# Squares and normalisation of queries and keys moved from GpSimd to VectorE in a one-core layer of attention and experts

## The chip, the cores and the metric

The kernel runs on one core of one Trainium2 chip. The metric is the device time of the kernel in microseconds, from one launch to its end; lower is better. A core has TensorE (PE, and PEld for its weight loads), VectorE (DVE), ScalarE (ACT), GpSimd (POOL) and SyncE (SP), which work side by side, each through its own list of instructions in program order. They wait for one another only on semaphores.

## What is computed

One layer over 16 sequences of 256 tokens with 128 features. The input is layer-normalised; two branches, a linear attention with random features and a mixture of soft-routed experts, are added to it.

```python
xn = _layernorm(x)                                   # 16 x 256 x 128
qkv = xn @ Wqkv + bqkv;  q, k, v = split(qkv, 3)     # 16 heads of 8
# features of q and of k:
u    = t / max(norm(t, axis=-1), 1e-12)              # per head of 8 numbers
proj = einsum('bhtd,rhdm->rbhtm', u, omega)          # 2 x 32 features
feat = exp(clip(proj * sqrt_2s - s, -20, 20)) / sqrt(32) * sqrt(weights)
# causal linear attention:
ctx = sum over earlier tokens of (q_f . k_f) v ;  den = max(sum (q_f . k_f), 1e-6)
attn = (ctx / den) @ Wout + bout
# soft mixture: logits of tokens and 512 slots, softmax over experts and over slots
slots = dispatch^T xn;  h = gelu(slots @ w1);  processed = h @ w2
ffn = combine @ processed
out = x + attn + ffn
```

The change touches `u`: the division of every head of 8 numbers of `q` and `k` by its norm.

## The kernel before

One pass of the loop (`row`, numbered 0 to 15 here) handles one sequence. Its 256 tokens lie as two tiles of 128. Every engine has its own `row` function, in which the steps stand in the order written by hand; nothing else sets the order. Passes 0 and 1 and the last two are written out, the twelve between run in a hardware loop of two passes (`run_rows`). In each function `b` is the pass, `b1` the next, `b2` the one after, `bp` the one before. Work is staggered: while pass `b` runs through the experts, its engines prepare queries, keys and values of `b1` and finish the attention of `bp`.

Queries and keys of `b1` go this way in pass `b`:

- TensorE makes `x23` = qkv (`qkv_product`), VectorE adds the bias and scales into `qkv` (`qkv_bias`, L758).
- `squares` (L322) writes `qk_sq` = qkv times qkv, 128x512. In the loop GpSimd does it. For pass 0, ahead of the loop, VectorE does.
- VectorE sums eights (`qk_norms`, L764) and applies a floor (L767).
- ScalarE takes the inverse root as Exp(-0.5 Ln) (`qk_root`, L525 and L527), and VectorE sharpens it with a Newton step of three instructions (`qk_newton`, L709, L711, L713, on 64 columns).
- `qk_apply` (L327) writes `qk_n` = qkv times the inverse norm, 128x512. In the loop on GpSimd, ahead of it on VectorE.
- ScalarE copies `qk_n` into `stack` in 16 bits (`stack_high`, L546), GpSimd writes the remainder (`stack_low`, L335), ScalarE copies once more (L677), SyncE turns the stack by a transposing DMA (`turn_stack`), and TensorE projects it in pass `b1` (`project`, L1014).

Around it: VectorE and ScalarE take score blocks out of PSUM (`evac_a`, L787, and `evac_b`, L559), GpSimd then multiplies half of them by a causal mask (`mask_b`, L476). VectorE's `slots_low` is L837, `clip` L781, `ctx_norm` starts with L795; `ln_newton` uses L709, L711 and L713 on four columns. ScalarE's functions Exp and Ln are in one table and Gelu is in another, so that a table load (L671) stands ahead of `gelu`. Its order in that part is

```python
evac_b(b, 2)
qk_root(b1)
evac_b(b, 3)
nc.scalar.preload_act_table_set(GELU)
gelu(b, 0)
stack_high(b1)
gelu(b, 1)
```

TensorE's `processed_low` (L1176) waits for `gelu(b, 0)`. In front of it stand `hidden` and `project(b, 2)`, `project(b, 3)`, and these two wait for `evac_a` and `evac_b` of blocks 2 and 3.

Of the kernel before, what the change touches and what calls it, by code (L numbers as in the profile page):

```python
# [34 lines left out]
def count(b, per, extra):  # L35

    i, u = b
    if isinstance(i, int):
        return (2 * i + u) * per + extra
    return i * (2 * per) + (u * per + extra)  # L40
# [8 lines left out]
def after(eng, sem, value):  # L49

    if isinstance(value, int) and value <= 0:
        return
    eng.wait_ge(sem, value)


def hold(eng, sem, value):

    if isinstance(value, int) and value <= 0:
        return
    eng.wait_ge(sem, value)  # L60
    eng.nop(nofuse=True)
# [7 lines left out]
def step(b, k):  # L69

    i, u = b
    u += k
    return (i + u // 2, u % 2)
# [19 lines left out]
def build(nc, x, Wqkv, bqkv, Wout, bout, omega, nodes, weights, gamma_x, gamma_slot, slot_embeds,  # L93
          w1, w2, out):
    with ExitStack() as ctx:
# [224 lines left out]
        def squares(eng, b):  # L320
            hold(eng, qkvs_ok, count(b, 1, 1))
            eng.tensor_tensor(qk_sq[:, :, :], qkv[:, :, 0:256], qkv[:, :, 0:256], ALU.mult).then_inc(sq_ok, 1)  # L322

        def qk_apply(eng, b):
            hold(eng, qk_nw, count(b, 3, 3))
            rn = small[:, NT, :].rearrange("p (j h a) -> p j h a", j=2, a=1).broadcast_to([128, 2, 32, HD])
            eng.tensor_tensor(qk_n[:, :, :].rearrange("p j (h d) -> p j h d", d=HD),  # L327
                              qkv[:, :, 0:256].rearrange("p j (h d) -> p j h d", d=HD), rn,
                              ALU.mult).then_inc(qkn_ok, 1)

        def stack_low(eng, b):
            hold(eng, sthi_ok, count(b, 1, 1))
            hold(eng, d_st, count(b, 16, 0))
            hold(eng, qkn_ok, count(b, 1, 1))
            eng.tensor_tensor(stacked(1), parted(), stacked(0), ALU.subtract).then_inc(stlo_ok, 1)  # L335
# [80 lines left out]
        def _(pool):  # L416
# [30 lines left out]
            def residual(b):  # L447

                hold(pool, d_x[b[1]], landed(b, 1))
                hold(pool, o1_ok, count(b, 1, -1))  # L450
                pool.tensor_tensor(xres[:, b[1], :, :], xin[:, b[1], :, :],
                                   bout_bc[:, :].rearrange("p (a c) -> p a c", a=1).broadcast_to([128, TILES, C]),
                                   ALU.add).then_inc(xr_ok, 1)

            def place_v(b):
                hold(pool, qkvs_ok, count(b, 1, 1))
                hold(pool, cx_ok, count(b, 4, -4))
                for a in range(4):
                    heads = slice(QUADS * a, QUADS * a + QUADS)
                    c = 256 + 32 * a  # L460
                    last = pool.tensor_copy(vw[:, b[1], :, heads, v_col(a):v_col(a) + HD],
                                            qkv[:, :, c:c + 32].rearrange("p j (h d) -> p j h d", d=HD))
                last.then_inc(v_ok, 1)

            def mask_pair(b, p):
                hold(pool, ev_ok, count(b, 2, p - 5))
                v = s_sb[:, p, :, :].rearrange("p k (a t) -> p k a t", t=128)[:, :, 0:3:2, :]
                m = causal[:, :].rearrange("p (k a t) -> p k a t", k=1, t=128)[:, :, 0:3:2, :].broadcast_to(
                    [128, 2, 2, 128])
                pool.tensor_tensor(v, v, m, ALU.mult).then_inc(mb_ok, 1)  # L470

            def mask_b(b, p):
                hold(pool, eb_ok, count(b, 6, p + 1))
                v = s_sb[:, p, 1, :].rearrange("p (a t) -> p a t", t=128)[:, 0:3:2, :]
                m = causal[:, :].rearrange("p (a t) -> p a t", t=128)[:, 0:3:2, :]
                pool.tensor_tensor(v, v, m, ALU.mult).then_inc(mb_ok, 1)  # L476
# [17 lines left out]
            def row(b, first, nxt, nxt2):  # L494
                b1, bp = step(b, 1), step(b, -1)
                if not first:
                    mask_pair(bp, 6)
                    mask_pair(bp, 7)
                if nxt:
                    residual(b1)  # L500
                    squares(pool, b1)
                mask_b(b, 0)
                mask_b(b, 1)
                if nxt:
                    qk_apply(pool, b1)
                    stack_low(pool, b1)
                mask_b(b, 2)
                mask_b(b, 3)
                if nxt:
                    place_v(b1)  # L510
                mask_b(b, 4)
                mask_b(b, 5)
# [192 lines left out]
        def _(dve):  # L705
            def newton(src, y, t, w, done, base, extra):

                ys, ts = small[:, y, 0:w], small[:, t, 0:w]
                nc.vector.scalar_tensor_tensor(ts, ys, -0.5, ys, ALU.mult, ALU.mult).then_inc(done, 1)  # L709
                after(dve, done, count(base, 3, extra - 2))  # L710
                nc.vector.tensor_tensor(ts, ts, small[:, src, 0:w], ALU.mult).then_inc(done, 1)  # L711
                after(dve, done, count(base, 3, extra - 1))
                nc.vector.scalar_tensor_tensor(ts, ts, 1.5, ys, ALU.add, ALU.mult).then_inc(done, 1)  # L713
                after(dve, done, count(base, 3, extra))
# [47 lines left out]
            def qk_norms(b):  # L762
                after(dve, sq_ok, count(b, 1, 1))
                nc.vector.tensor_reduce(small[:, NQ, :], qk_sq[:, :, :].rearrange("p j (h d) -> p (j h) d", d=HD),  # L764
                                        AX_X, ALU.add).then_inc(red_ok, 1)
                after(dve, red_ok, count(b, 2, 1))
                nc.vector.tensor_scalar(small[:, NM, :], small[:, NQ, :], NORM_FLOOR, None,  # L767
                                        ALU.max).then_inc(red_ok, 1)

            def qk_newton(b):  # L770
                after(dve, qk_a, count(b, 2, 2))
                after(dve, red_ok, count(b, 2, 2))
                newton(NM, NY, NT, 64, qk_nw, b, 3)
# [45 lines left out]
            def slot_maxima(b):  # L819

                for h in range(2):
                    after(dve, lt_ok, count(b, 2, h + 1))
                    nc.vector.tensor_reduce(maxima[:, 2 * h:2 * h + 2], x23[:, h, :].rearrange("p (c t) -> p c t", t=T),  # L823
                                            AX_X, ALU.max).then_inc(mx_ok, 1)
# [34 lines left out]
            b0, b1 = (0, 0), (0, 1)  # L859
# [47 lines left out]
            def row(b, first, nxt, nxt2):  # L907

                b1, b2, bp = step(b, 1), step(b, 2), step(b, -1)
                token_maxima(b)  # L910
                if first:
                    ln_stats(b1)
                slot_maxima(b)
                if first:
                    dve.wait_ge(f_ln, 1)
                    nc.vector.tensor_tensor(f_bias[:, :], coef_ln[:, :], node_c[:, :], ALU.subtract).then_inc(f_ok, 1)
                    ln_newton(b1)
                    ln_scale(b1)
                elif nxt2:
                    ln_stats(b2)  # L920
                clip(b, 0)
                slots_norm(b, 0)
                slots_norm(b, 1)
                if first:
                    xt_low(b1)
                clip(b, 1)
                if first:
                    ln_stats(b2)
                if first:
                    slots_low(b)  # L930
                if nxt:
                    qkv_bias(b1)
                evac_a(b, 0)
                evac_a(b, 1)
                if not first:
                    slots_low(b)
                if nxt:
                    qk_norms(b1)
                evac_a(b, 2)
                evac_a(b, 3)  # L940
                if nxt:
                    qk_newton(b1)
                if nxt2:
                    ln_newton(b2)
                if nxt2:
                    ln_scale(b2)
                clip(b, 2)
                if not first and nxt:
                    ctx_norm(bp)
                clip(b, 3)  # L950
                if nxt:
                    add_experts(b)
                else:
                    ctx_norm(bp)
                if nxt2:
                    xt_low(b2)
                if not first and nxt:
                    add_attention(bp)
                evac_a(b, 4)
                evac_a(b, 5)  # L960
# [366 lines left out]
```

## Time and profile before

| | before |
|---|---|
| median of 3 runs | 450.51 us (449.58 to 450.86) |
| the profiled execution | 450.92 us |
| its span, first to last instruction | 449.2 us |
| mean granted TensorE clock | 0.995 |
| TensorE (matmul) busy | 431.4 us, 96% |
| VectorE busy | 348.2 us, 78% |
| ScalarE busy | 319.3 us, 71% |
| GpSimd busy | 188.8 us, 42% |

The span is what the instructions cover in the profiled execution; the 1.7 us beside it lie around them. Busy time is a share of the whole span and doesn't say who waits for whom: for that the timelines below are read. In a line of a timeline stand the start and the length in us, the engine, the line of the kernel, the operation, what it writes and reads, the shapes, and how many instructions were merged into it. In brackets, if anything, the idle time of the engine ahead of it and who ended it. A start can lie a little ahead of the end of the instruction before on the same engine, since they overlap in the pipeline.

### The profile page before, as it was taken

The page shows a single profiled execution, that of the slowest core. Times are in us where ns is not written, and L with a number is a line of the kernel's source. Part 1 is how long each engine was busy: PE and PEld are TensorE (multiplying, and loading weights), DVE is VectorE, ACT ScalarE, POOL GpSimd, SP SyncE. Part 2 cuts the span into 40 slices and gives each one's busy share as a digit, 9 for nine tenths or more (in the row PEclk, how much of TensorE's full clock was granted, in tenths as well). Part 3 has the DMA queues.
Part 4 walks back from the last instruction along what each step waited for, and adds up shares of the span by engine and source line. Part 5 has one row for each costly group of instructions (what it writes and reads, how often), then busy time and mean ns, then how long its engine had stood idle before and what let it go on. Part 6 is the DMA issues. An engine that isn't in the chain of part 4 may idle for free.

```text
span 449.2 us, 15766 instructions
## 1 busy us (share of the span) xinstructions
PE 431.4 (96%) x5724; PEld 361.5 (80%) x5724; DVE 348.2 (78%) x872; ACT 319.3 (71%) x530; POOL 188.8 (42%) x280
## 2 busy tenths in 40 slices
PE   6688999999999999999999999999999999999986
PEld 3467888898888889888888988888898888889775
DVE  7797797978778697877969787796978779576643
ACT  4458686877958687685868768586876858676671
POOL 5605454344445434434643443464344346434310
PEclk9899999999999999999999999999999999999999
DMA  4302003030200203020020302002030201103001
GB/s 108 88 25 49 14 4 60 14 60 16 47 26 8 51 12 58 12 47 23 13 46 12 58 12 47 23 17 41 12 58 12 47 12 24 36 1 61 2 1 25
DMA packets 45307, 14.37 MB, mean 32 GB/s; under 512 B 35360, under 2 KB 45152, under 8 KB 45280
## 3 DMA queue, kind: packets, MB, share of 16 engines
q1 hardware_dynamic: 44432, 13.48, 14.6%
q10 hardware_dynamic: 720, 0.53, 0.4%
q8 instruction: 17, 0.28, 0.2%
q0 software_dynamic: 128, 0.01, 0.1%
q14 instruction: 10, 0.08, 0.1%
HBM read 3.44 MB, written 2.10 MB: 12 GB/s over the span
## 4 chain that ended last, share of the span: by engine, by line
PE 90%; DVE 6%; ACT 2%; issue 1%; POOL 0%; DVEq 0%; ACTq 0%; POOLq 0%
PE x L979 19%; PE p_s L1029 10%; PE p_t L1029 8%; PE x L1176 7%; PE x L1144 7%; PE x L1185 6%; PE x L1197 6%; PE x L1042 5%; PE p_s L1042 5%; PE x L1117 3%; PE p_s L1014 2%; PE x L1128 2%; PE x L1093 2%; PE x L1152 2%; PE x L1136 1%; PE x L1081 1%
## 5 line engine op out<-in xcount | busy, mean ns | idle before, releaser
L476 POOL TENSOR_TENSOR s_sb<-s_sb,causal 128x256 f32<-128x256 f32 x96 | 68.5, 734 | 82.5 <-ACT s_sb L559 82.4
L553 ACT ACTIVATE feat<-arg,f_bias 128x1024 f32<-128x1024 f32 x64 | 71.7, 1147 | 8.0 <-DVE arg L781 8.0
L781 DVE TENSOR_SCALAR arg<-p_s,f_low,f_high 128x1024 f32<-128x1024 f32 x32 | 42.9, 1340 | 18.6 <-PE p_s L1014 12.1
L1029 PEld LDWEIGHTS p_s<-feat 64*64 64x64 f32 x1024 | 38.8, 132 | 17.4 <-issue 15.8
L322 POOL TENSOR_TENSOR qk_sq<-qkv 128x512 f32<-128x512 f32 x15 | 15.6, 1042 | 86.8 <-DVE qkv L758 86.8
L1029 PE MATMUL p_s<-feat 64*64 64x256 f32 (+3 forms) x1024 | 49.5, 309 | 1.6 <-ACT feat L553 1.6
L470 POOL TENSOR_TENSOR s_sb<-s_sb,causal 128x512 f32<-128x512 f32 x30 | 37.6, 1276 | 26.5 <-ACT s_sb L565 26.5
L1029 PE MATMUL p_t<-feat 64*64 64x256 f32 (+3 forms) x1024 | 47.1, 299 | 0.0
L781 DVE TENSOR_SCALAR arg<-p_t,f_low,f_high 128x1024 f32<-128x1024 f32 x32 | 42.7, 1335 | 0.0
L1029 PEld LDWEIGHTS p_t<-feat 64*64 64x64 f32 x1024 | 41.3, 133 | 1.5
L1176 PEld LDWEIGHTS x<-w_sb,hid_t 128*128 128x128 f32 x256 | 29.8, 191 | 8.5 <-ACT hid_t L593 8.0
L1144 PEld LDWEIGHTS x<-xg,disp 128*128 128x128 f32 x256 | 29.8, 191 | 7.9 <-ACT disp L581 7.9
L559 ACT ACTIVATE s_sb<-p_s 128x384 f32<-128x384 f32 x48 | 23.6, 491 | 15.8 <-PE p_s L1029 15.8
L1176 PE MATMUL x<-w_sb,hid_t 128*128 128x128 f32 x256 | 32.8, 281 | 1.7 <-ACT hid_t L593 1.7
L823 DVE TENSOR_REDUCE maxima<-x 128x2 bf16<-128x512 f32 x32 | 20.6, 686 | 17.0 <-PE x L1117 16.9
L1144 PE MATMUL x<-xg,disp 128*128 128x129 f32 x256 | 32.8, 281 | 0.2
L593 ACT ACTIVATE hid_t<-x 128x1024 f32<-128x1024 f32 x32 | 32.7, 1021 | 0.3
L565 ACT ACTIVATE s_sb<-p_s 128x768 f32<-128x768 f32 x15 | 12.2, 813 | 28.2 <-PE p_s L1029 28.2
L1197 PE MATMUL x<-proc,comb_t 128*128 128x129 f32 x256 | 31.6, 275 | 0.0
L1185 PE MATMUL x<-w_sb,hid_t 128*128 128x128 f32 x256 | 31.2, 275 | 0.0
L1197 PEld LDWEIGHTS x<-proc,comb_t 128*128 128x128 f32 x256 | 29.9, 191 | 0.3 <-issue 0.2
L1185 PEld LDWEIGHTS x<-w_sb,hid_t 128*128 128x128 f32 x256 | 29.8, 192 | 0.0
(162 smaller groups left out, 1038.9 us busy)
## 6 DMA issues: line engine op xcount, KB each, us to landing
xin<-in_L_attn_x_dram SPq DMA_DIRECT2D x31, 64.0 KB, 2.3
out_dram<-out_sb SPq DMA_DIRECT2D x31, 64.0 KB, 2.1
se_rows<-n_L_ffn_slot_embeds_dram SPq DMA_DIRECT2D x1, 256.0 KB, 4.1
w_f<-in_L_ffn_w_dram SPq DMA_DIRECT2D x1, 256.0 KB, 4.0
w_sb<-in_L_ffn_w_dram SPq DMA_DIRECT2D x1, 256.0 KB, 3.9
stack_t<-stack SPq DMA_TRANSPOSE x16, 4.3
wqkv_f<-in_L_attn_Wqkv_dram ACTq DMA_DIRECT2D x1, 192.0 KB, 2.9
bqkv_bc<-in_L_attn_bqkv_dram ACTq DMA_DIRECT2D x1, 192.0 KB, 4.9
```

The lines of the kernel that those rows point to most:

```text
L470: pool.tensor_tensor(v, v, m, ALU.mult).then_inc(mb_ok, 1)
L476: pool.tensor_tensor(v, v, m, ALU.mult).then_inc(mb_ok, 1)
L553: nc.scalar.activation(feat[:, k:k + 2, :], arg[:, k:k + 2, :], ACT.Exp, bias=f_bias[:, 0:1]).then_inc(fe_ok, 1)
L593: nc.scalar.activation(hid_t[:, 2 * half:2 * half + 2, :], (x01, x23)[half][:, :, :], ACT.Gelu).then_inc(ge_ok, 1)
L781: nc.vector.tensor_scalar(arg[:, k:k + 2, :], (p_s, p_t)[g % 2][:, :, :], f_low[:, 0:1], f_high[:, 0:1], ALU.max, ALU.min).then_inc(cl_ok, 1)
L979: mm = nc.tensor.matmul(dst, a, w, start=start and i == 0, stop=stop and i == 2, skip_group_check=True)
L1029: mm = nc.tensor.matmul(dst[rows:rows + 64, u, o:o + hi - lo], f[:, T + keys:T + keys + 64], f[:, lo:hi], start=True, stop=True, skip_grou ...
L1042: mm = nc.tensor.matmul(dst[32 * q:32 * q + 32, j, :], vw[:, b[1], kt, QUADS * a + q, :], s_sb[:, p, q % 2, o:o + 128], start=(kt == 0 and ...
L1144: mm = nc.tensor.matmul(x01[:, half, 129 * (c % 2):129 * (c % 2) + 129], disp[:, j, 128 * c:128 * c + 128], xg[:, b[1], j, :], start=(j == ...
L1176: nc.tensor.matmul(x01[:, c // 2, o:o + 128], hid_t[:, m, 128 * c:128 * c + 128], w2_sb[:, m, :], start=(m == 0 and c % 2 == 0), stop=Fals ...
L1185: mm = nc.tensor.matmul(x01[:, c // 2, o:o + 128], hid_t[:, m, 128 * c:128 * c + 128], w2_sb[:, m, :], start=False, stop=(m == 3), skip_gr ...
L1197: mm = nc.tensor.matmul(x23[:, 0, 129 * j:129 * j + 129], comb_t[:, c, 128 * j:128 * j + 128], proc[:, c, :], start=(c == 0 and j == 0), s ...
```

## The change

On VectorE, `squares` now stands behind `evac_a(b, 1)` and, in all passes but 0, `slots_low`, directly in front of `qk_norms`. `qk_apply` stands directly behind `qk_newton`, in front of `ln_newton` of the pass after next. Both are gone from GpSimd's list. The instructions are the same, in operands and shape; only the engine and the place differ. Both helpers begin with an explicit wait and an empty instruction (`hold`).

```diff
@@ GpSimd, row
                 if nxt:
                     residual(b1)
-                    squares(pool, b1)
                 mask_b(b, 0)
                 mask_b(b, 1)
                 if nxt:
-                    qk_apply(pool, b1)
                     stack_low(pool, b1)
                 mask_b(b, 2)
                 mask_b(b, 3)
@@ VectorE, row
                 if not first:
                     slots_low(b)
                 if nxt:
+                    squares(dve, b1)
                     qk_norms(b1)
                 evac_a(b, 2)
                 evac_a(b, 3)
                 if nxt:
                     qk_newton(b1)
+                    qk_apply(dve, b1)
                 if nxt2:
                     ln_newton(b2)
```

VectorE's list in a pass before, from the second evacuation to the four-column Newton (`small` holds the norms and roots, `s_sb` the evacuated scores):

```order
L787 TENSOR_TENSOR s_sb<-p_t,causal 128x384
L837 TENSOR_TENSOR slot_lo<-x,slot_hi 128x512
L764 TENSOR_REDUCE small<-qk_sq 128x64
L767 TENSOR_SCALAR small<-small 128x64
L787 TENSOR_TENSOR s_sb<-p_s,causal 128x384
L787 TENSOR_TENSOR s_sb<-p_t,causal 128x384
L709 SCALAR_TENSOR_TENSOR small<-small 128x64
L711 TENSOR_TENSOR small<-small 128x64
L713 SCALAR_TENSOR_TENSOR small<-small 128x64
L709 SCALAR_TENSOR_TENSOR small<-small 128x4
```

Here the sums (L764) follow `slots_low` (L837) directly, and one Newton step the other. The same piece after the change, whose line numbers are two lower from the edit on:

```order
L785 TENSOR_TENSOR s_sb<-p_t,causal 128x384
L835 TENSOR_TENSOR slot_lo<-x,slot_hi 128x512
L322 TENSOR_TENSOR qk_sq<-qkv 128x512
L762 TENSOR_REDUCE small<-qk_sq 128x64
L765 TENSOR_SCALAR small<-small 128x64
L785 TENSOR_TENSOR s_sb<-p_s,causal 128x384
L785 TENSOR_TENSOR s_sb<-p_t,causal 128x384
L707 SCALAR_TENSOR_TENSOR small<-small 128x64
L709 TENSOR_TENSOR small<-small 128x64
L711 SCALAR_TENSOR_TENSOR small<-small 128x64
L327 TENSOR_TENSOR qk_n<-qkv,small 128x512
L707 SCALAR_TENSOR_TENSOR small<-small 128x4
```

The squares have come between `slots_low` and the sums, ahead of the floor; the multiply has come between the two Newton steps.

GpSimd's list at the same place of a pass, as a difference from before:

```order
 L470 TENSOR_TENSOR s_sb<-s_sb,causal 128x2x2x128 x2
 L451 TENSOR_TENSOR xres<-xin,bout_bc 128x256
-L322 TENSOR_TENSOR qk_sq<-qkv 128x512
 L476 TENSOR_TENSOR s_sb<-s_sb,causal 128x2x128 x2
-L327 TENSOR_TENSOR qk_n<-qkv,small 128x512
 L335 TENSOR_TENSOR stack<-qk_n,stack 128x32x16
 L476 TENSOR_TENSOR s_sb<-s_sb,causal 128x2x128 x2
```

The masks 0 and 1 (L476) no longer stand behind the squares, and `stack_low` (L335) follows them directly. The lists of TensorE, ScalarE and SyncE are unchanged.

## Rows read from the trace of the kernel before

**Rows 1.** The page's busy time; busy time by stretch (columns: PE, PEld, DVE, ACT, POOL, PEclk).

```profile
PE 431.4 (96%) x5724; PEld 361.5 (80%) x5724; DVE 348.2 (78%) x872; ACT 319.3 (71%) x530; POOL 188.8 (42%) x280
...
30.00:40.00 10.00, 7.76 (x92) 5.79 (x91) 9.33 (x27) 7.16 (x13) 3.98 (x5) 1.00 0.00 0
```

**Rows 2.** Timeline of pass 7, TensorE's weight loads for `processed_low`.

```profile
220.53 1.64 PEld L1176 LDWEIGHTS x<-w_sb,hid_t 128*128 128x128 f32 x14 [0.42 <-ACT hid_t L593]
```

**Rows 3.** Timeline of pass 7, VectorE: `slots_low`, sums, floor, four-column Newton, `ctx_norm`.

```profile
215.34 0.68 DVE L837 TENSOR_TENSOR slot_lo<-x,slot_hi 128x512 fp32r<-128x512 f32 x1
215.94 0.68 DVE L764 TENSOR_REDUCE small<-qk_sq 128x64 f32<-128x512 f32 x1
216.65 0.46 DVE L767 TENSOR_SCALAR small<-small 128x64 f32<-128x64 f32 x1
...
218.90 1.03 DVE L709 SCALAR_TENSOR_TENSOR small<-small 128x4 f32<-128x4 f32 x1 [0.21 <-DVE small L713]
...
223.05 0.27 DVE L795 TENSOR_SCALAR den<-x 128x16 f32<-128x16 f32 x2 [0.47 <-PE x L1081]
```

**Rows 4.** Timeline of pass 7, ScalarE: second evacuation, logarithm, first Gelu.

```profile
215.23 0.48 ACT L559 ACTIVATE s_sb<-p_t 128x384 f32<-128x384 f32 x1
...
217.14 0.26 ACT L525 ACTIVATE small<-small 128x64 f32<-128x64 f32 x1
...
219.38 1.02 ACT L593 ACTIVATE hid_t<-x 128x1024 f32<-128x1024 f32 x1
```

**Rows 5.** Timeline of pass 7, GpSimd: squares, masks 0 and 1, multiply.

```profile
214.64 1.04 POOL L322 TENSOR_TENSOR qk_sq<-qkv 128x512 f32<-128x512 f32 x1 [5.40 <-DVE qkv L758]
215.63 1.42 POOL L476 TENSOR_TENSOR s_sb<-s_sb,causal 128x256 f32<-128x256 f32 x2
218.83 1.08 POOL L327 TENSOR_TENSOR qk_n<-qkv,small 128x512 f32<-128x512 f32 x1 [1.78 <-DVE small L713]
```

**Rows 6.** Timeline of pass 0: ScalarE, VectorE and TensorE's loads, engine by engine.

```profile
32.98 0.48 ACT L559 ACTIVATE s_sb<-p_t 128x384 f32<-128x384 f32 x1
...
37.72 1.02 ACT L593 ACTIVATE hid_t<-x 128x1024 f32<-128x1024 f32 x1
...
34.77 0.68 DVE L767 TENSOR_SCALAR small<-small 128x64 f32<-128x64 f32 x1
...
37.07 0.16 DVE L709 SCALAR_TENSOR_TENSOR small<-small 128x4 f32<-128x4 f32 x1
...
38.79 1.30 PEld L1176 LDWEIGHTS x<-w_sb,hid_t 128*128 128x128 f32 x11 [2.11 <-ACT hid_t L593]
```

**Rows 7.** Timeline of pass 8: ScalarE, VectorE and TensorE's loads, engine by engine.

```profile
241.45 0.48 ACT L559 ACTIVATE s_sb<-p_t 128x384 f32<-128x384 f32 x1
...
245.51 1.03 ACT L593 ACTIVATE hid_t<-x 128x1024 f32<-128x1024 f32 x1
...
241.47 0.68 DVE L837 TENSOR_TENSOR slot_lo<-x,slot_hi 128x512 fp32r<-128x512 f32 x1
...
242.78 0.46 DVE L767 TENSOR_SCALAR small<-small 128x64 f32<-128x64 f32 x1
...
246.70 0.41 PEld L1176 LDWEIGHTS x<-w_sb,hid_t 128*128 128x128 f32 x3 [0.42 <-ACT hid_t L593]
```

**Rows 8.** Timeline of the prologue: VectorE's squares, floor, multiply; GpSimd's addition.

```profile
10.84 0.69 DVE L322 TENSOR_TENSOR qk_sq<-qkv 128x512 f32<-128x512 f32 x1
...
12.29 0.20 DVE L767 TENSOR_SCALAR small<-small 128x64 f32<-128x64 f32 x1
...
15.62 0.72 POOL L451 TENSOR_TENSOR xres<-xin,bout_bc 128x256 f32<-128x256 f32 x1
...
15.88 1.02 DVE L327 TENSOR_TENSOR qk_n<-qkv,small 128x512 f32<-128x512 f32 x1
```

**Rows 9.** Timeline ahead of pass 7: ScalarE's evacuation and GpSimd's pair of masks.

```profile
202.29 0.49 ACT L559 ACTIVATE s_sb<-p_s 128x384 f32<-128x384 f32 x1 [0.46 <-PE p_s L1029]
...
202.93 1.44 POOL L476 TENSOR_TENSOR s_sb<-s_sb,causal 128x256 f32<-128x256 f32 x2 [4.51 <-ACT s_sb L559]
```

## The prediction

> **What bounds the kernel now.** I read the page first, then the granted clock by stretches, then the timelines of single passes of the loop. TensorE is busy 96% of the span [rows 1], and most of the chain that ended last is its own. So an edit on VectorE and GpSimd costs or gives only where TensorE waits for something behind it, and the question is which wait that is. The edited work is squares of queries and keys, their sums, a floor, a root on ScalarE, Newton steps, and the multiply. In the timelines of pass 7 the reader can follow who hangs on the floor (L767). It ends at 217.11 [rows 3] and ScalarE's logarithm (L525) starts at 217.14 [rows 4]: no slack. ScalarE works in program order: behind the root stand one evacuation, a table load and the Gelu of the first half, 219.38 to 220.40. TensorE's weight loads for `processed_low` (L1176) start at 220.53, released by that Gelu [rows 2]. How much room is in those 0.13 us? In pass 0, where TensorE truly waited (2.11 us), the load came 0.05 us after the Gelu's end (37.72 + 1.02 = 38.74, load 38.79) [rows 6]. So pass 7 has 0.08 us of room. Pass 8 ends its Gelu at 246.54 and loads at 246.70: room 0.11 us [rows 7]. **A later floor is a later TensorE, in every pass with a next row, less about 0.1 us.**
>
> **Squares, removed from GpSimd.** L322 on GpSimd takes 1.04 us, 214.64 to 215.68 [rows 5]. It ran beside two evacuations and `slots_low` on VectorE, which end only at 215.34 + 0.68 = 216.02 [rows 3]. The sums started at 215.94, straight behind them, and waited for no square. So the removed 1.04 us lay wholly beside other work and gives VectorE nothing back at this place.
>
> **Squares, added to VectorE.** The same instruction ran once on VectorE in the prologue, with GpSimd idle: 0.69 us [rows 8]. In the loop it stands between `slots_low` and the sums, on the chain above. It meets company, because GpSimd's masks come earlier once the squares are gone from its queue. When GpSimd is idle, a mask starts about 0.14 us after its evacuation by ScalarE ends: 202.29 + 0.49 = 202.78, and the mask at 202.93 [rows 9]. In pass 7 the second evacuation ends at 215.71 [rows 4], so the second mask runs from 215.85 for 0.73 us (a pair takes 1.42, slightly overlapped [rows 5]) to 216.58. VectorE reaches the squares at about 216.05. What does a VectorE instruction with two operands in SBUF do while GpSimd multiplies SBUF by SBUF? Two rows answer. L709 on four columns takes 0.16 us alone [rows 6] and 1.03 us when it starts 0.07 us behind GpSimd's `qk_n`, ending 0.02 us after it (219.93 against 218.83 + 1.08 = 219.91) [rows 3, 5]. The prologue's L327, a multiply of the very size of the squares, started at 15.88 under GpSimd's addition (15.62 to 16.34) and ended at 16.90, 0.56 us after it [rows 8]. So I let the squares end 0.56 us after the mask.
>
> The new chain from the end of ScalarE's second evacuation is then 0.14 (to the mask) + 0.73 (mask) + 0.56 (squares) + 0.04 (to the sums) + 0.68 (sums [rows 3]) + 0.04 + 0.20 (floor) = 2.39 us. The 0.04 is the gap that sums and floor leave now (215.94 + 0.68 to 216.65 [rows 3]), and 0.20 is the floor's free length in the prologue [rows 8]; in the loop it takes 0.46, as the mask holds it, and that is gone too. **Pass 7**: 215.71 + 2.39 = 218.10 against 217.11, 0.99 late, 0.91 after the room. **Pass 8**: the evacuation ends at 241.93, so 244.32 against 242.78 + 0.46 = 243.24, 1.08 late, 0.97 after the room [rows 7]. The odd passes look like pass 7, the even ones like pass 8. **Pass 0**: the evacuation ends at 33.46, so 35.85 against 34.77 + 0.68 = 35.45: 0.40 late with no room, since TensorE waits there anyway [rows 6]. Pass 15 has no next row and nothing changes. The sum is 7 x 0.91 + 7 x 0.97 + 0.40 = 13.6 us.
>
> Bounds of the added squares: from below 0.69 us without any block; from above the whole 0.69 behind the mask instead of 0.56, which adds 0.13 x 15 = 2 us.
>
> The Trainium skill has the rule: in "SBUF — State Buffer", section "Who interferes with whom", a VectorE instruction with two SBUF inputs contends with a GpSimd instruction that reads SBUF, and whichever issues first holds the shared pair for its whole length. By it the squares would start only at the mask's end and take their full length, 13.6 + 2 = 15.6 us. The row of L327 ended sooner, so the measurement decides for 0.56.
>
> **Multiply, removed from GpSimd and added to VectorE.** On GpSimd `qk_n` ran 218.83 to 219.91 [rows 5]. On VectorE it stands behind the Newton steps. GpSimd is idle by then, its next step waits for ScalarE's `stack_high`, so no block: between the 0.69 us of the squares' size and the 1.02 us that L327 took under a block [rows 8]; I take 0.7, since nothing contends. Measured from the same late floor, `qk_n` is ready no later than before (218.9 + 0.7 = 219.6 against 219.91). Its reader, ScalarE's copy, stands behind the Gelu that ends at 220.40 [rows 4], so even 1.02 us is covered; without that cover each 0.1 us would be another 0.1 us on ScalarE. On VectorE it pushes the four-column Newton by 0.7 us and takes away the 0.87 us for which GpSimd's `qk_n` held it (1.03 against 0.16). Net -0.1 to +0.2 us ahead of `clip(b, 2)`. Behind it VectorE waits 0.47 us for TensorE's transposes (L795 [rows 3]), which covers that. **Cost nothing.**
>
> **What else waits.** The evacuations `evac_a` 2 and 3 come about 1 us later. Today they and the 64-column Newton are over by 218.9, where the four-column one starts [rows 3]; `project(b, 2)` and `(b, 3)` want them just ahead of L1176, at about 220, so they still come in time. `stack_low` on GpSimd waits for the same ScalarE copy as before. Masks 0 and 1 come earlier, for nobody. No DMA is moved; the stack's transpose on SP shifts with ScalarE as TensorE does, and its reader stands in the next pass.
>
> Nothing gives the lateness back: ScalarE's whole queue behind the root moves with it, and TensorE's later waits in the pass are for that queue or for its own results. Does TensorE's clock hold? Between 30 and 40 us it was busy only 7.76 of 10 us and was granted 1.00 [rows 1], so another 0.9 us of idling should not change it.
>
> The profiled execution took 450.92 us (span 449.2 and 1.7 us around it), 0.4 above the median 450.51. 450.92 + 13.6 - 0.4 = 464.1; I say **464.0 us**.
>
> **Rivals.** (1) *VectorE reaches the squares before the mask.* Then the mask waits and the squares take 0.69. How near is it? If the squares need no time beyond the queue, they start where the sums do now: 215.94 against the mask's 215.85 in pass 7, and 242.07 against 242.07 in pass 8. The explicit wait ahead of the squares should add some 0.1 us: the sums, which have no such step, start 0.08 us before `slots_low` ends, and an engine that runs an extra empty instruction first (my estimate) loses that overlap. That speaks for the mask, and 0.07 us behind was enough for L709 to be held. Price: 216.05 + 0.69 + 0.04 + 0.68 + 0.04 + 0.20 = 217.70, 0.59 late, 0.5 after the room; 14 x 0.5 + 0.4 = 7.4, so 457.9 us if in all passes, 461 if only in the even ones.
>
> (2) *Lateness absorbed* (not slower). If `processed_low` were really held by the projections in front of it and the root's chain had a microsecond of slack, or if TensorE's stall shortened its later waits, the added 0.69 us would vanish: 450.5 us. For it: TensorE's matmuls fill 96% of the span, so little of this wait shows as idle. Against: the loads follow the Gelu by only 0.13 and 0.16 us [rows 2, 7].
>
> (3) *Faster.* If what TensorE waits for is not the Gelu but VectorE's second half (`xg`, `clip(b, 2)`, `ctx_norm`), then ending the block of 0.87 us for a multiply of 0.7 gives 0.15 us in each of 14 passes: 450.5 - 2.1 = 448.4 us. It decides only where VectorE arrives last; the wait of 0.47 us at L795 says it does not. The Trainium skill leans this way: "GPSIMD Engine Reference", section "Engine selection", sends elementwise work on two inputs to VectorE since GpSimd is about twice as slow. The rows agree on the ratio (1.04 against 0.69), but it prices the instruction, not its place.
>
> (4) *Worse than forecast*: the clock falls, or a second stall opens, for instance at `attn_back`: 467 us and more.
>
> **How the numbers follow.** Forecast (mask first in nearly all passes, 462 to 466) 0.62; rival 1, in part or whole, 457 to 462, 0.20; absorbed 0.08; faster 0.04; worse 0.06. The range reaches from rival 1 in all passes, with 1 us for its terms, to the full block: 457 to 467, leaving out under 0.2. A measurement of this kernel tells 0.3% (1.4 us) from no change. Faster 0.04, same 0.07, slower 0.89.
>
> **What would show it.** In the changed profile: VectorE's L322 near 1.1 us (0.53 waiting for the mask and 0.56) and not 0.69; the floor near 0.2; ScalarE's L525 waiting some 1 us for it; loads of L1176 with idle of 1.3 us in place of 0.42, released by the Gelu; a pass of 27.1 us in place of 26.17 (220.53 to 246.70); the four-column Newton at 0.16. Wrong if L1176 waits as before, if L322 takes 0.69, or if the pass stays at 26.2.

## The result and the profile after

The changed kernel took 462.12 us (median of 4 runs, 461.98 to 462.27) against 450.69 us for the kernel before, run beside it: a ratio of 1.0253, 95% interval 1.0224 to 1.0281. It is 11.4 us slower; 13.5 us were forecast, with a range of 457 to 467. The profiled execution took 461.99 us with a span of 460.3 us.

The page of the changed kernel, its busy times and three of its groups (columns: instructions, busy us, mean ns of one, idle us ahead and who ended it):

```profile
PE 434.2 (94%) x5724; PEld 363.2 (79%) x5724; DVE 357.1 (78%) x902; ACT 319.6 (69%) x530; POOL 162.2 (35%) x250
...
L476 POOL TENSOR_TENSOR s_sb<-s_sb,causal 128x256 f32<-128x256 f32 x96 | 72.4, 769 | 175.3 <-ACT s_sb L557 175.3
...
L1176 PEld LDWEIGHTS x<-w_sb,hid_t 128*128 128x128 f32 x256 | 31.4, 200 | 17.9 <-ACT hid_t L591 17.5
...
L1176 PE MATMUL x<-w_sb,hid_t 128*128 128x128 f32 x256 | 34.4, 290 | 10.3 <-ACT hid_t L591 10.3
```

TensorE's share fell from 96% [rows 1] to 94%, GpSimd's from 42% to 35%, and VectorE stays at 78% of a longer span. GpSimd gave away 27 us of work for which another engine had waited only once, VectorE for 0.29 us in pass 0. TensorE's idle time ahead of L1176 is where the loss is: the matmuls there waited 1.7 us for the Gelu in the whole kernel before, all of it in pass 0, and 10.3 us now.

Pass 7 of the changed kernel, VectorE first, then ScalarE, GpSimd and TensorE's loads (timeline; it answers to rows 2 to 5; line numbers from the edit on are two lower):

```profile
220.84 0.68 DVE L835 TENSOR_TENSOR slot_lo<-x,slot_hi 128x512 fp32r<-128x512 f32 x1
221.44 1.20 DVE L322 TENSOR_TENSOR qk_sq<-qkv 128x512 f32<-128x512 f32 x1
222.67 0.69 DVE L762 TENSOR_REDUCE small<-qk_sq 128x64 f32<-128x512 f32 x1
223.39 0.19 DVE L765 TENSOR_SCALAR small<-small 128x64 f32<-128x64 f32 x1
...
225.36 0.69 DVE L327 TENSOR_TENSOR qk_n<-qkv,small 128x512 f32<-128x512 f32 x1
225.97 0.15 DVE L707 SCALAR_TENSOR_TENSOR small<-small 128x4 f32<-128x4 f32 x1
...
229.46 0.27 DVE L793 TENSOR_SCALAR den<-x 128x16 f32<-128x16 f32 x2 [0.69 <-PE x L1081]
...
223.62 0.26 ACT L523 ACTIVATE small<-small 128x64 f32<-128x64 f32 x1 [1.01 <-DVE small L765]
...
225.86 1.02 ACT L591 ACTIVATE hid_t<-x 128x1024 f32<-128x1024 f32 x1
...
221.36 0.73 POOL L476 TENSOR_TENSOR s_sb<-s_sb,causal 128x256 f32<-128x256 f32 x1 [0.68 <-ACT s_sb L557]
...
226.93 1.86 PEld L1176 LDWEIGHTS x<-w_sb,hid_t 128*128 128x128 f32 x16 [1.33 <-ACT hid_t L591]
```

The mask starts at 221.36, the squares 0.08 us behind it. The mask ends at 222.09 and the squares at 222.64, 0.55 us later: they were held. ScalarE then waits 1.01 us for the floor, and TensorE's loads 1.33 us for the Gelu. They had idled 0.42 us before [rows 2], under matmuls that were still running; the matmuls of L1176 themselves idled 0.00 us before and 0.84 us now. The multiply takes 0.69 us and the four-column Newton behind it 0.15 us, where it had been held for 1.03 [rows 3].

Pass 8 of the same profile, VectorE, GpSimd and TensorE's loads:

```profile
248.48 0.68 DVE L322 TENSOR_TENSOR qk_sq<-qkv 128x512 f32<-128x512 f32 x1
...
249.91 0.20 DVE L765 TENSOR_SCALAR small<-small 128x64 f32<-128x64 f32 x1
...
248.48 1.27 POOL L476 TENSOR_TENSOR s_sb<-s_sb,causal 128x256 f32<-128x256 f32 x1 [0.68 <-ACT s_sb L557]
...
253.45 1.86 PEld L1176 LDWEIGHTS x<-w_sb,hid_t 128*128 128x128 f32 x16 [0.77 <-ACT hid_t L591]
```

Here both start at 248.48 and VectorE wins. The squares take their free 0.68 us, and the mask, 0.73 alone, takes 1.27. TensorE's loads wait only 0.77 us. Six of the 14 later passes with a next row (2, 4, 6, 8, 10, 12) went this way, eight (the odd ones and pass 14) the other. The mean of the mask group shows it too: 769 ns against 734 before, and 6 x 0.54 us over 96 masks is 34 ns.

Distance between the first loads of L1176 in neighbouring passes, from the timelines:

| kernel | into pass 7 | into pass 8 |
|---|---|---|
| before | 26.06 | 26.17 |
| the whole change | 26.97 | 26.52 |
| squares only | 26.98 | 26.51 |
| multiply only | 26.06 | 26.16 |
| change, mask 1 behind the squares | 26.55 | 26.62 |
| change, block 3 evacuated first | 26.60 | 26.17 |
| change, mask 1 behind the floor, block 3 first | 26.06 | 26.16 |
| before, block 3 first | 26.07 | 26.15 |
| change, multiply twice | 26.95 | 26.52 |
| squares twice | 26.67 | 26.74 |

### The profile page after: what moved, and what is told of

Same layout as the page of the kernel before. It is cut to its first block, busy times and chain, and to the rows that moved or that the text cites. A ratio compares the mean times of both kernels' runs of the same rounds, so it can differ in the third digit from the quotient of the medians.

```text
span 460.3 us, 15753 instructions
## 1 busy us (share of the span) xinstructions
PE 434.2 (94%) x5724; PEld 363.2 (79%) x5724; DVE 357.1 (78%) x902; ACT 319.6 (69%) x530; POOL 162.2 (35%) x250
## 4 chain that ended last, share of the span: by engine, by line
PE 61%; DVE 19%; ACT 9%; issue 8%; DMA 1%; DVEq 1%; ACTq 0%
PE x L1176 7%; PE x L979 7%; PE x L1144 7%; PE x L1185 6%; PE x L1197 6%; PE p_s L1029 5%; PE p_s L1042 5%; PE p_t L1029 4%; ACT hid_t L591 3%; PE x L1117 3%; DVE qk_sq L322 3%; DVE qkv L756 3%; ACT L669 3%; DVE small L762 2%; DVE s_sb L785 2%
## 5 line engine op out<-in xcount | busy, mean ns | idle before, releaser
L476 POOL TENSOR_TENSOR s_sb<-s_sb,causal 128x256 f32<-128x256 f32 x96 | 72.4, 769 | 175.3 <-ACT s_sb L557 175.3
L1029 PEld LDWEIGHTS p_s<-feat 64*64 64x64 f32 x1024 | 38.8, 132 | 17.4 <-issue 15.9
L470 POOL TENSOR_TENSOR s_sb<-s_sb,causal 128x512 f32<-128x512 f32 x30 | 37.6, 1276 | 26.8 <-ACT s_sb L563 26.8
L1176 PEld LDWEIGHTS x<-w_sb,hid_t 128*128 128x128 f32 x256 | 31.4, 200 | 17.9 <-ACT hid_t L591 17.5
L335 POOL TENSOR_TENSOR stack<-qk_n,stack 128x512 f16<-128x512 f32 x15 | 17.5, 1165 | 77.2 <-ACT stack L544 77.2
L1176 PE MATMUL x<-w_sb,hid_t 128*128 128x128 f32 x256 | 34.4, 290 | 10.3 <-ACT hid_t L591 10.3
L1144 PE MATMUL x<-xg,disp 128*128 128x129 f32 x256 | 32.8, 281 | 0.2
L1185 PE MATMUL x<-w_sb,hid_t 128*128 128x128 f32 x256 | 31.2, 275 | 0.0
L1185 PEld LDWEIGHTS x<-w_sb,hid_t 128*128 128x128 f32 x256 | 29.9, 192 | 0.0
```

Source lines behind the costliest of these rows:

```text
L1029: mm = nc.tensor.matmul(dst[rows:rows + 64, u, o:o + hi - lo], f[:, T + keys:T + keys + 64], f[:, lo:hi], start=True, stop=True, skip_grou ...
L1144: mm = nc.tensor.matmul(x01[:, half, 129 * (c % 2):129 * (c % 2) + 129], disp[:, j, 128 * c:128 * c + 128], xg[:, b[1], j, :], start=(j == ...
L1176: nc.tensor.matmul(x01[:, c // 2, o:o + 128], hid_t[:, m, 128 * c:128 * c + 128], w2_sb[:, m, :], start=(m == 0 and c % 2 == 0), stop=Fals ...
L1185: mm = nc.tensor.matmul(x01[:, c // 2, o:o + 128], hid_t[:, m, 128 * c:128 * c + 128], w2_sb[:, m, :], start=False, stop=(m == 3), skip_gr ...
```

## Where the 11.1 us of span went

By the first loads of L1176 in both profiles, the loss adds up to the difference of the spans. Passes into which the mask came first: 0.91 us each for 3, 5, 7, 9, 11 and 13, 0.93 for 14 and 0.95 for 1 (by the profile of the squares alone, whose clock was full there), together 7.3. Passes where VectorE came first: 0.32 to 0.35 each, together 2.0. Pass 0: 0.14 as the profiles stand; it holds 0.25 us by which this execution came earlier to the loop (see **Pass 0** below). That is 9.5 us. The remaining 1.6 us is TensorE's clock, once. This is TensorE of the changed kernel by stretches around its wait in pass 0 (columns: us, PE busy, granted clock, DMA share, GB/s):

```profile
36.00:38.00 2.00, 1.04 (x6) 1.00 0.00 0
38.00:39.00 1.00, 0.07 (x1) 0.95 0.00 0
39.00:42.00 3.00, 3.00 (x14) 0.50 0.00 0
42.00:43.00 1.00, 1.00 (x10) 0.85 0.92 171
```

From 39 to 42 us it was granted half of the full clock (1.2 GHz in place of 2.4), just behind the wait for the first Gelu. Of the 16 matmuls of L1176 in pass 0, thirteen took 0.42 us each by their own length in place of 0.28, which is why the group L1176 is busy 34.4 us in place of 32.8. The profile of the kernel before had the same wait (2.11 us [rows 6]) and kept its full clock there.

## The experiments

Each kernel was profiled and then timed beside the kernel before on the same chip. In the first set of four the kernel before had a median of 451.29 us (14 runs), in the second 451.12 us (19 runs). All single times move by 1 to 3 us with the mean granted clock of the run: the kernel before took 449.5 to 449.9 us at 0.998 to 0.999 and 452.6 to 453.1 at 0.986 to 0.987. Part of this lies ahead of the loop. The profile of the kernel before was below the full clock there (columns as above):

```profile
15.00:20.00 5.00, 2.72 (x8) 0.80 0.08 18
20.00:25.00 5.00, 4.39 (x27) 0.85 0.65 128
```

It reached the first load of L1176 at 38.79 us. The profiles with the full clock up to there reached it at 37.1 to 37.8, the ones without at 38.8 to 39.9, whatever the kernel. So the distances between loads above, which leave all this out, carry the arguments, and the medians confirm them.

### The two halves of the change

Only the squares on VectorE, against the changed kernel:

```diff
@@ GpSimd, row
                 if nxt:
+                    qk_apply(pool, b1)
                     stack_low(pool, b1)
@@ VectorE, row
                     qk_newton(b1)
-                    qk_apply(dve, b1)
```

> Only the squares are on VectorE; the multiply stays with GpSimd, behind masks 0 and 1. My theory (all of the loss comes from the squares in front of the floor, the multiply is covered): the same as with the whole change, 462 us, within 1.5 us, with the squares again near 1.20 us in odd passes and 0.68 in even ones, and the four-column Newton again held for some 0.87 us by the multiply on GpSimd. Rival (both instructions cost VectorE their length on the path, 0.69 us each): half of the loss goes, about 456 us.

Measured: 461.57 us (ratio to before 1.0239, 1.019 to 1.0287). Pass 7, VectorE, GpSimd, loads:

```profile
220.23 1.20 DVE L322 TENSOR_TENSOR qk_sq<-qkv 128x512 f32<-128x512 f32 x1
...
224.24 1.02 DVE L708 SCALAR_TENSOR_TENSOR small<-small 128x4 f32<-128x4 f32 x1 [0.21 <-DVE small L712]
...
224.18 1.07 POOL L327 TENSOR_TENSOR qk_n<-qkv,small 128x512 f32<-128x512 f32 x1 [3.29 <-DVE small L712]
...
225.73 1.42 PEld L1176 LDWEIGHTS x<-w_sb,hid_t 128*128 128x128 f32 x12 [1.33 <-ACT hid_t L592]
```

The squares are held and TensorE's loads wait 1.33 us exactly as in the whole change, while the four-column Newton is held again by the multiply. This block of 0.87 us changes nothing for TensorE.

Only the multiply on VectorE, against the changed kernel:

```diff
@@ GpSimd, row
                     residual(b1)
+                    squares(pool, b1)
@@ VectorE, row
-                    squares(dve, b1)
                     qk_norms(b1)
```

> Only the multiply is on VectorE; the squares stay with GpSimd in front of masks 0 and 1. My theory: it costs nothing, as the Gelu that its reader stands behind ends later and the block of the four-column Newton goes: 450.7 us, within 1 us, loads of L1176 idle 0.42 us as before. Rival (both cost their length): about 456 us or, if it is all the multiply's, 462 us.

Measured: 451.66 us, ratio 1.0001 (0.9978 to 1.0023). Pass 7:

```profile
218.74 0.69 DVE L327 TENSOR_TENSOR qk_n<-qkv,small 128x512 f32<-128x512 f32 x1
219.35 0.16 DVE L708 SCALAR_TENSOR_TENSOR small<-small 128x4 f32<-128x4 f32 x1
...
220.45 1.64 PEld L1176 LDWEIGHTS x<-w_sb,hid_t 128*128 128x128 f32 x14 [0.42 <-ACT hid_t L592]
```

The multiply is free, and ending the block gains nothing either. The whole loss belongs to the squares.

### Is the 1.20 us a block?

The whole change, with mask 1 waiting for the squares:

```diff
@@ GpSimd, row
                 mask_b(b, 0)
+                if nxt:
+                    hold(pool, sq_ok, count(b1, 1, 1))
                 mask_b(b, 1)
```

> The whole change, but GpSimd waits for the squares before mask 1, so that VectorE is first in every pass. My theory (in 8 of 14 passes and in pass 0 the mask holds the squares for 0.5 us): squares 0.68 us in all passes, all passes 26.5 us, 14 x 0.35 = 5 us above before and 0.4 us back in pass 0: 455.3 us, or 457 if the clock falls in pass 0 again. Rival (the 1.20 us is VectorE's own time, not a block; only the added instruction counts): squares stay at 1.20 in odd passes and the time at 462 us.

Measured: 457.48 us (ratio 1.0144, 1.0099 to 1.0189). Pass 7, VectorE and GpSimd:

```profile
217.43 0.68 DVE L322 TENSOR_TENSOR qk_sq<-qkv 128x512 f32<-128x512 f32 x1
...
218.86 0.30 DVE L767 TENSOR_SCALAR small<-small 128x64 f32<-128x64 f32 x1
...
218.37 0.74 POOL L476 TENSOR_TENSOR s_sb<-s_sb,causal 128x256 f32<-128x256 f32 x1 [1.70 <-DVE qk_sq L322]
```

The squares take 0.68 us in every pass, so the 0.5 us was the mask's. Passes became 26.55 and 26.62 us, not the 26.5 that was expected. The rows tell why: the mask now runs from 218.37 to 219.11 over the floor, which is held until 219.16 and takes 0.30 us in place of 0.20. I had moved the collision by one instruction. In pass 14 the overlap was worse and the floor took 0.55 us. That is why 455.3 us was too low: even the profiled execution, at the full clock, took 456.42.

### Is it floor, root, table load, Gelu?

The whole change, with ScalarE's order turned, so that block 3 is evacuated in the time in which ScalarE waits for the floor:

```diff
@@ ScalarE, row
                 evac_b(b, 2)
+                evac_b(b, 3)
                 if nxt:
                     qk_root(b1)
-                evac_b(b, 3)
```

> The whole change, but ScalarE evacuates block 3 ahead of the root instead of behind it, in the time in which it waits for the floor. My theory (the path is floor, root, table load, Gelu, processed_low): the Gelu comes 0.47 us earlier against the floor, so 0.91 becomes 0.44 in the odd passes and 0.34 becomes 0 in the even ones: 8 x 0.45 and 0.3 us less in pass 0, some 454 us, 455.6 if the clock falls as with the change. Rival (VectorE as a whole is late, and the root is not what TensorE hangs on): 462 us as before.

Measured: 455.81 us (ratio 1.0102, 1.0068 to 1.0136). ScalarE in pass 7, and the loads of passes 7 and 8:

```profile
220.96 0.49 ACT L557 ACTIVATE s_sb<-p_t 128x384 f32<-128x384 f32 x1
221.91 0.26 ACT L523 ACTIVATE small<-small 128x64 f32<-128x64 f32 x1 [0.47 <-DVE small L765]
...
223.77 1.02 ACT L591 ACTIVATE hid_t<-x 128x1024 f32<-128x1024 f32 x1
...
224.85 1.30 PEld L1176 LDWEIGHTS x<-w_sb,hid_t 128*128 128x128 f32 x11 [0.94 <-ACT hid_t L591]
...
251.02 1.08 PEld L1176 LDWEIGHTS x<-w_sb,hid_t 128*128 128x128 f32 x9 [0.42 <-ACT hid_t L591]
```

From the logarithm to the Gelu it is 1.86 us in place of 2.24 (223.62 to 225.86), 0.38 earlier and not 0.47. The odd passes fell from 0.91 to 0.54 above before, the even ones to nothing. VectorE's list is unchanged, so TensorE hangs on ScalarE's queue behind the floor and not on VectorE's second half. This profile also had the clock at half behind the wait of pass 0, the one of squares only had not.

Both mends together, with the mask behind the floor (`hold(pool, red_ok, count(b1, 2, 2))` in place of the wait above) and block 3 first:

> The whole change, with GpSimd's mask 1 waiting for VectorE's floor and with ScalarE's block 3 evacuated ahead of the root. My theory (late by the added squares less the ended hold of the floor, 1.63 against 1.17 us = 0.46; 0.38 given back by ScalarE's order, 0.08 to 0.11 by the room): nothing is left, passes of 26.1 us, the time of the kernel before within 1 us, the floor at 0.20 us and loads of L1176 idle 0.42. Rival (VectorE's longer list costs by itself): at least 0.3 us a pass remains, 455 us or more.

Measured: 450.30 us, ratio 0.9982 (0.9964 to 0.9999). Pass 7, VectorE and loads:

```profile
214.29 0.69 DVE L322 TENSOR_TENSOR qk_sq<-qkv 128x512 f32<-128x512 f32 x1
...
215.73 0.20 DVE L767 TENSOR_SCALAR small<-small 128x64 f32<-128x64 f32 x1
...
218.89 1.19 PEld L1178 LDWEIGHTS x<-w_sb,hid_t 128*128 128x128 f32 x10 [0.43 <-ACT hid_t L593]
```

Nothing is left of the loss, though VectorE does all that it does in the changed kernel. The kernel before with ScalarE's order turned alone tells whether this order is a gain of its own:

> The kernel before, with only ScalarE's order turned (block 3 ahead of the root). My theory: TensorE reaches the loads of L1176 with the Gelu just done, so an earlier Gelu gives it nothing: the time of before within 1 us, so what this order gave in the changed kernel was lateness taken back. Rival (the order is a gain of its own): 5 us faster than before.

Measured: 449.85 us, ratio 0.998 (0.996 to 0.9999). Its loads in pass 7 and in pass 0:

```profile
218.88 1.30 PEld L1176 LDWEIGHTS x<-w_sb,hid_t 128*128 128x128 f32 x11 [0.42 <-ACT hid_t L593]
...
37.14 1.53 PEld L1176 LDWEIGHTS x<-w_sb,hid_t 128*128 128x128 f32 x13 [1.74 <-ACT hid_t L593]
```

The passes stay at 26.07 and 26.15 us. Only in pass 0, where TensorE truly waits, the Gelu's earlier end counts: 1.74 in place of 2.11 us. Runs at a mean clock of 0.998 and more agree: 449.1 to 449.4 us here, 449.3 with both mends, 449.5 to 449.9 for the kernel before. Both are some 0.4 us (0.1%) faster than before; the rest of the difference of medians goes with the clock of the runs. No version was found that beats the kernel before by more than that.

### Doubling one, doubling the other

The whole change, with the multiply done once more into the free `qk_sq`, ahead of the real one. In the diff `qk_again` is the multiply of `qk_apply` without wait and signal:

```diff
@@ VectorE, row
                     qk_newton(b1)
+                    qk_again(b1)
                     qk_apply(dve, b1)
```

> The whole change, with the multiply done twice on VectorE, one behind the other. My theory (qk_n ends 0.8 us ahead of the Gelu that ScalarE's copy stands behind, and VectorE waits 0.69 us for TensorE's transposes behind clip): 0.70 us more in front of both is still covered, 462 us, within 1.5 us, and the wait ahead of L793 shrinks to near 0. Rival (the multiply is on the path): 0.7 x 15 = 10 us more, 472 us.

Measured: 461.25 us (ratio 1.0216, 1.0181 to 1.0251). Pass 7, VectorE:

```profile
224.76 0.69 DVE L333 TENSOR_TENSOR qk_sq<-qkv,small 128x512 f32<-128x512 f32 x1
225.37 0.69 DVE L327 TENSOR_TENSOR qk_n<-qkv,small 128x512 f32<-128x512 f32 x1
...
228.96 0.27 DVE L798 TENSOR_SCALAR den<-x 128x16 f32<-128x16 f32 x2 [0.17 <-PE x L1087]
```

A second multiply costs nothing: the passes stay at 26.95 and 26.52 us. VectorE's wait for the transposes shrank from 0.69 to 0.17 us: that is the cover, and it is nearly used up.

The kernel with both mends, with the squares done twice (first into the spare tile `junk`, with the same wait):

```diff
@@ VectorE, row
                 if nxt:
+                    sq_again(b1)
                     squares(dve, b1)
                     qk_norms(b1)
```

> As the first kernel of this set (mask 1 behind the floor, block 3 ahead of the root), but the squares are computed twice on VectorE, the first time into a spare tile. It does work that the reference does not ask for. My theory (once the room is used up, what stands in front of the floor costs its length): 0.69 to 0.72 us a pass, 10 us above the first kernel, 461 us, passes of 26.8 us. Rival (slack elsewhere takes it): under 3 us above.

Measured: 459.81 us (ratio 1.0193, 1.0166 to 1.0221), 9.5 us above the kernel with both mends. Pass 7, VectorE and loads:

```profile
220.10 0.69 DVE L333 TENSOR_TENSOR junk<-qkv 128x512 f32<-128x512 f32 x1
220.70 0.69 DVE L322 TENSOR_TENSOR qk_sq<-qkv 128x512 f32<-128x512 f32 x1
...
225.31 1.86 PEld L1183 LDWEIGHTS x<-w_sb,hid_t 128*128 128x128 f32 x16 [1.04 <-ACT hid_t L597]
```

Two in a row overlap by 0.09 us, so the second adds 0.60 us and not the 0.69 to 0.72 of the theory, and the passes grew by 0.61 and 0.58 (26.67 and 26.74, 26.8 expected). Once the room is gone, what stands in front of the floor costs its full step, pass after pass. The profile lost another 1.6 us behind pass 0's wait, where the clock was at half.

## Why the prediction was right, and where it was off

**What bounds the kernel.** Right. Turning ScalarE's order took the even passes back to 26.17 us without an edit on VectorE, and the squares alone carried the whole loss.

**Squares: GpSimd's 1.04 us gives nothing back.** Right for the loop: with the multiply alone on VectorE and with the squares alone, TensorE's loads moved only by what came in front of the floor. In pass 0 of the kernel before, VectorE's sums did wait 0.29 us for GpSimd's squares. The forecast for pass 0 starts at the evacuation and ends at the measured floor, so it has this wait in it.

**The length of held squares.** Right to 0.01 us: 0.55 us past the mask's end, 0.56 predicted from the prologue. From the evacuation's end (221.22) to the floor's end (223.58) the chain took 2.36 us, 2.39 predicted, and the odd passes cost 0.91 us each, as predicted. The squares took 1.20 us and not 1.1, as they began to wait 0.1 us sooner. The full length behind the mask, which the Trainium skill ("SBUF — State Buffer", "Who interferes with whom") would give, was 0.14 us too long. What the Trainium skill states there besides, that the first to issue keeps the other out, agrees with the odd passes, where the mask started 0.08 us ahead. In the even passes the two starts agree to 0.01 us, and no row tells who was first.

**Who comes first in the even passes.** This is the step that failed. I took the explicit wait and its empty instruction ahead of the squares for 0.1 us, so that the mask would win everywhere. They cost nothing: the squares start 0.60 us behind the start of `slots_low` (220.84 to 221.44), just as the sums had (215.34 to 215.94 [rows 3]). Without the 0.1 us the sum in rival 1 stood at a tie in pass 8, 242.07 against 242.07, and VectorE won it, as in all six passes where the starts agree to 0.01 us. Why it wins such a tie is open. One of the prediction's own signs of being wrong, L322 at 0.69 us, came true in these six. The even passes then cost 0.34 us in place of 0.97: 6 x 0.63 = 3.8 us too much in the forecast. Rival 1 had this case, "only in the even ones", at 461 us.

**Pass 0.** The floor came 2.37 us after the evacuation's end in place of 1.99 (33.46 to 35.45 before), 0.38 later against 0.40 predicted. It cost only 0.14 us in the profile, since ScalarE reached that evacuation 0.25 us sooner, for reasons ahead of the loop. In the profile of the squares alone, where the evacuation ended at 33.46 as before, the floor and the loads of L1176 both came 0.39 us later (35.84, and 39.18 against 38.79). So the step was right.

**The multiply costs nothing.** Right, and by more than one way: alone it gives the time of before, and twice it still costs nothing.

**TensorE's clock.** Wrong. I read from one stretch with the full clock that another wait would not lower it. In the profile it fell behind pass 0's wait and cost 1.6 us. All four runs of the changed kernel had a mean clock of 0.988 to 0.991. The kernel before had 0.986 to 0.999; its profile (0.995) was below the full clock ahead of the loop and not here, and where its other runs were, no trace shows. So it isn't shown that the change makes the fall likelier: the profile of the squares alone has the same wait of pass 0 and kept the full clock. The run of the doubled multiply at 0.999 took 459.44 us, 9.5 to 9.9 more than the kernel before at 0.998 to 0.999; that is the cost of the change with the clock left out, and the 9.4 us of passes 1 to 14 with 0.4 for pass 0 give it.

**The sum.** With 3.8 us too much for the even passes, 0.3 too much for pass 0 and 1.6 too little for the clock, the sum of 13.6 us stood 2.5 above the 11.1 us of the spans. The errors leaned against each other; how near the total came is partly luck.

**Rivals.** "Absorbed" falls with the 1.33 and 0.77 us of idle ahead of L1176. "Faster" falls with the multiply alone, which ended the block of 0.87 us and gained nothing. The prediction took GpSimd's 1.04 us against 0.69 for an agreement with "about twice as slow"; it is a factor of 1.5.

## What to carry to other kernels

Before moving an instruction from an idle engine to a busy one, ask who waits for its result, not what it takes: in the loop the squares were free on GpSimd, though 1.5 times as long there, because they ended under other VectorE work, and on VectorE 0.69 us stood in front of a root, a table load and a Gelu that TensorE waits for. Taking work off GpSimd also lets its other work start sooner, here just onto the moved instruction. When a late result can't be made earlier, let its waiting engine do independent work first: one swapped line on ScalarE gave back 0.34 to 0.37 us a pass.

## What the runs showed of the hardware beyond the expected

- VectorE with two operands in SBUF and GpSimd multiplying in SBUF exclude each other both ways, though no semaphore stands between them. Started at the same time by the profile (248.48), VectorE kept 0.68 us and GpSimd's mask grew from 0.73 to 1.27, ending 0.59 us behind the squares; 0.08 us behind the mask, the squares grew to 1.20. Held work ends sooner than its full length after the release: 0.55 of 0.69 and 0.59 of 0.73.
- An explicit wait that is already satisfied and an empty instruction in front of a VectorE instruction did not move its start (0.60 us from the start of the instruction before, with and without).
- TensorE's loads waited 2.11 or 2.12 us in pass 0 in the profiles of before, of the change, of the squares alone, of the multiply alone, of mask 1 behind the squares and of the doubled multiply, and TensorE's clock fell behind the wait only in that of the change. It also fell with the order turned (wait of 1.73 us) and with squares twice (1.74), but not with both mends (1.77) or in the kernel before with the order turned (1.74). What decides this was not settled; the length of the wait alone does not. Each fall there costs 1.6 us, which is as much as 0.35% of this kernel.
